# Score bursts without first-layer units, the bias folded into the score matmuls, and a ring of ten activation buffers

## The reference

```python
x = x + attention(layernorm(x))      # 8 heads of 16 channels, 768 x 768 scores
t = t + ffn(layernorm(t))            # t: the same tokens
# attention: softmax(q k / 4 + time_bias[tk - tq] + part_bias[nk - nq]) v, causal in the time
att = att + bias_t + bias_p
att = jnp.where(causal, att, -jnp.inf); att = softmax(att); y = (att @ v) @ Wo
# ffn: two scaled copies of x (top-2 of 8 gate probabilities, normalised), all 8 experts
top_p = top_p / sum(top_p)
for i in range(2):
    h = gelu(einsum('btd,edf->ebtf', x * top_p[..., i:i+1], W1) + b1)
    out = out + einsum('ebtf,efd->btd', h, W2) + b2_sum
```

## Time and profile before

| what | value |
|---|---|
| median of 3 runs | 2730.64 us |
| profiled execution | 2739.47 us, its span 2737.6 us |
| TensorE busy | 2377.7 us (87%), granted clock 0.957 |
| ScalarE busy | 1695.3 us (62%) |
| VectorE busy | 1469.6 us (54%) |
| GpSimd busy | 1089.9 us (40%) |
| first second-layer unit starts (end of the prologue) | 228.5 us |
| last round | 2656.8 to 2737.6 us, 80.8 us |

### The profile page before, as it was taken

One profiled execution on the slowest core, in us unless ns is written; L12 is line 12 of the kernel. 1 busy time (PEld: TensorE's weight loads), 2 busy tenths in 40 slices (PEclk: granted clock), 3 DMA queues, 4 the chain that ended last, 5 costly groups with the idle time before them and its releaser, 6 DMA issues.

```text
span 2737.6 us, 57322 instructions
## 1 busy us (share of the span) xinstructions
PE 2377.7 (87%) x18611; PEld 2127.1 (78%) x18611; DVE 1469.6 (54%) x4157; ACT 1695.3 (62%) x2788; POOL 1089.9 (40%) x1054
## 2 busy tenths in 40 slices
PE   1567989899898989989899898989989898998989
PEld 0347878788887878888787878878887787888878
DVE  7536365444735545474554636544573554547454
ACT  2125656675675666666566665667566566756667
POOL 6004244343433434343343424434352443434347
PEclk9678999999999999999999999999999999999999
DMA  2411212040221303022030212203022120302200
GB/s 34 73 38 25 28 28 34 7 52 7 31 28 20 42 7 43 13 34 28 10 49 10 31 25 34 28 8 51 10 28 28 24 38 7 44 12 34 28 10 7
DMA packets 62802, 74.34 MB, mean 27 GB/s; under 512 B 16192, under 2 KB 43744, under 8 KB 62432
## 3 DMA queue, kind: packets, MB, share of 16 engines
q1 hardware_dynamic: 62528, 70.68, 18.4%
HBM read 11.19 MB, written 6.29 MB: 6 GB/s over the span
## 4 chain that ended last, share of the span: by engine, by line
PE 57%; DVE 17%; issue 13%; ACT 9%; DMA 2%; POOL 1%; SPq 1%; DVEq 0%; POOLq 0%; ACTq 0%
PE acc L904 15%; PE wide L827 6%; PE narrow L844 6%; PE zps L893 6%; ACT z L504 5%; PE wide L830 5%; DVE wide L656 5%; PE zps L895 4%; PE zps L894 4%; PE wide L811 4%; DVE h L727 2%; PE wide L865 2%; PE wide L851 1%; DMA stack<-stack 1%; DVE maxes L656 1%
## 5 line engine op out<-in xcount | busy, mean ns | idle before, releaser
L445 POOL TENSOR_TENSOR hsum<-h 128x384 f32<-128x384 f32 x1024 | 1030.2, 1010 | 1491.9 <-ACT h L533 1477.3
L727 DVE TENSOR_TENSOR h<-zps,ratio_b 128x384 f32<-128x384 f32 x1024 | 561.8, 555 | 921.1 <-PE zps L895 917.3
L532 ACT ACTIVATE h<-zps,b_col 128x384 f32<-128x384 f32 x1024 | 594.3, 580 | 662.4 <-DVE h L727 637.1
L904 PE MATMUL acc<-w,hsum 128*128 128x128 f32 x6144 | 867.3, 278 | 1.4 <-DVE outt L736 1.2
L904 PEld LDWEIGHTS acc<-w,hsum 128*128 128x128 f32 x6144 | 850.2, 195 | 2.2 <-POOL hsum L445 1.7
L533 ACT ACTIVATE h<-h,b_col 128x384 f32<-128x384 f32 x1024 | 620.7, 606 | 0.0
L893 PE MATMUL zps<-x_hi,w_lo 128*128 128x384 f32 x1024 | 426.5, 416 | 100.7 <-ACT h L532 57.6
L656 DVE CUSTOM_DVE_ANT_0 wide<-wide,query_table 128x768 f32<-128x768 f32 (+5 forms) x768 | 461.6, 649 | 46.7 <-PE wide L811 44.0
L827 PE MATMUL wide<-stack 128*128 128x256 f32 (+3 forms) x1280 | 374.7, 323 | 69.9 <-ACT z L504 33.9
L504 ACT ACTIVATE z<-wide 128x896 f32<-128x896 f32 (+2 forms) x384 | 345.3, 918 | 95.1 <-PE wide L830 94.3
L894 PE MATMUL zps<-x_lo,w_hi 128*128 128x384 f32 x1024 | 353.4, 345 | 0.0
(11 more groups left out here) (110 smaller groups left out, 1609.2 us busy)
## 6 DMA issues: line engine op xcount, KB each, us to landing
stack<-halves SPq DMA_DIRECT2D x512, 96.0 KB
x_in<-in_x SPq DMA_DIRECT2D x136, 48.0 KB, 2.4
out_dram<-outt SPq DMA_DIRECT2D x256, 24.0 KB, 1.6
stack<-stack SPq DMA_DIRECT2D x128, 6.0 KB
z<-in_L_ffn_W SPq DMA_DIRECT2D x8, 256.0 KB, 4.2
stack<-max_rows SPq DMA_DIRECT2D x64, 12.0 KB
bias_rows<-w_hi SPq DMA_DIRECT2D x1, 192.0 KB
bias_rows<-w SPq DMA_DIRECT2D x1, 192.0 KB
```

What stands on the lines that cost most here:

```text
L445: pool.tensor_tensor(hsum[:, m % NHS, :], h0[:, m % 2, :], h1[:, m % NH1, :], ALU.add).then_inc(hsum_ready, 1)
L532: act.activation(h0[:, m % 2, :], zps[m % 2][:, 0:CT], ACT.Gelu, bias=b1_col[:, j:j + 1]).then_inc(h0_ready, 1)
L727: vec.tensor_tensor(h1[:, m % NH1, :], zps[m % 2][:, 0:CT], ratio_b[:, c * CT:(c + 1) * CT], ALU.mult).then_inc(z1_ready, 1)
L904: ins = pe.matmul(acc[:, n * P:(n + 1) * P], hsum[:, k % NHS, n * P:(n + 1) * P], w2[:, j, :], start=(j == 0 and n == 0), stop=(j == UNITS ...
```

## The change

- **Schedule.** Slots 20 to 25 and 41 to 46 get no first-layer unit; twelve other slots (`DOUBLE`) get two. So the first layer leads by 4 up to slot 5, by 10 after slots 16 and 37, and by 4 again after each burst. The twelve score steps of a group are spread two a slot over a burst. `query`, `key`, `value` move to slots 1, 2, 3 (from 2, 2, 4), the first maxima to slot 6 (from 8), `mix` to `project` to 47..51 (from 44..49), `split` of chunk 1 to slot 62 (from 60).
- **Ring.** `hsum` is gone: GpSimd adds `h0` into `h1` in place. `h1` has ten places; `ring_places()` gives the 64 units turns of 10, 9, 9, 9, 9, 9, 9 places. VectorE's product of unit m now waits for the second-layer unit m - BACK[m]; BACK is 9 for m = 0 to 8 and for every m from 19 on, 10 for m = 10 to 18, and 64 for m = 9.
- **Bias.** `qst` has a row block for each of the 8 heads with 768 + 384 columns; three products of halves take 48 rows, the bias tables and their one-hot keys rows 48 to 126, the maxima row 127. So one matmul gives scores with bias, for maxima and for scores; VectorE's maximum is a plain `tensor_reduce`. `rows` keeps the high half alone. Each `stack` step has six DMAs instead of five, `rows` eight instead of two.
- **Gate.** top-2 weights by tanh of half the difference of the two largest logits, instead of exp and sums.
- **Prologue.** Other bias tables, W1 staged in `w2`'s place earlier.

```diff
-NHS = 4
-STACK_DMAS = 5
+BURSTS = (20, 41)
+BURST = 6
+DOUBLE = (6, 8, 10, 12, 14, 16, 27, 29, 31, 33, 35, 37)
+RING = 10
...
+    plan += maxima(0, (6, 7, 8, 9, 10, 11, 12, 13, 14, 15, 16, 16)) + [(17, "rows", 0)]
...
+FIRSTS = [0 if any(b <= k < b + BURST for b in BURSTS) else 2 if k in DOUBLE else 1 for k in range(UNITS)]
+def ring_places():
+    turns = next([RING] * n + [RING - 1] * ((UNITS - RING * n) // (RING - 1)) for n in range(UNITS)
+                 if (UNITS - RING * n) % (RING - 1) == 0)
+    return [n for turn in turns for n in range(turn)]
+PLACE = ring_places()
+BACK = [next(d for d in range(1, UNITS + 1) if PLACE[m - d] == PLACE[m]) for m in range(UNITS)]
...
+                m = LAG
                 for k in range(UNITS):
                     steps(k, False)
-                    if k + LAG < UNITS:
-                        unit(this, k + LAG)
...
+                    for _ in range(FIRSTS[k]):
+                        if m < UNITS:
+                            unit(this, m)
+                        elif following:
+                            unit(following, m - UNITS)
+                        m += 1
                     after(this, k)
...
-                    for n, (q, k) in enumerate(((0, 2), (1, 2), (0, 3), (1, 3))):
+                    for n, (q, k) in enumerate(((0, 2), (1, 2), (0, 3))):
...
+                    for n, q in enumerate((0, 1, 0)):
+                        sp.dma_start(qst[n * HD:(n + 1) * HD, h, TOK:QW].bitcast(F32),
+                                     halves[rows, q, HALF:TOK]).then_inc(stack_loaded[hh], 16)
...
                 pool.wait_ge(h1_ready, r.at(UNITS, m + 1))
-                pool.wait_ge(hsum_used, r.at(UNITS, m + 1))
-                pool.tensor_tensor(hsum[:, m % NHS, :], h0[:, m % 2, :], h1[:, m % NH1, :],
+                pool.tensor_tensor(h1[:, PLACE[m], :], h0[:, m % 2, :], h1[:, PLACE[m], :],
...
-                    act.activation(gate_e[:, :, :], shifted[:, :, :], ACT.Exp).then_inc(gate_exped, 1)
+                    act.activation(gate_t[:, :], gate_d[:, :], ACT.Tanh, scale=0.5).then_inc(gate_exped, 1)
...
-                        ins = vec.tensor_tensor_reduce(w[:, at:at + n], w[:, at:at + n],
-                                                       query_table[:, h, TOK - n:TOK], 1.0, -3e38, ALU.add, ALU.max,
...
+                        ins = vec.tensor_reduce(maxes[:, hh * TILES + i:hh * TILES + i + 1], w[:, at:at + (i + 1) * P], AX.X, ALU.max)
...
-                vec.wait_ge(hsum_ready, r.at(UNITS, m + 1))
-                vec.tensor_tensor(h1[:, m % NH1, :], zps[m % 2][:, 0:CT], ratio_b[:, c * CT:(c + 1) * CT],
+                vec.wait_ge(hsum_used, r.at(UNITS, m + 1 - BACK[m] + UNITS))
+                vec.tensor_tensor(h1[:, PLACE[m], :], zps[m % 2][:, 0:CT], ratio_b[:, c * CT:(c + 1) * CT],
...
-                        ins = pe.matmul(w[:, at:at + q1 - q0], key_hot[:, g, :], bias_rows[:, hh, q0 - i * P:q1 - i * P],
-                                        start=False, stop=True)
+                        shift = HALF if i >= HT else 0
+                        ins = pe.matmul(w[:, at:at + q1 - q0], kst[:, hh, i * P:(i + 1) * P],
+                                        qst[:, g * GH + hh, q0 + shift:q1 + shift], start=True, stop=True)
```

More of the change, by code:

```diff
@@ L50, in maxima, with scores @@
         return [(slot, "maxima", (g, n // 3, n % 3)) for n, slot in enumerate(slots)]
+    def scores(g, at):
+        return [(at + n // 2, "scores", (g, n // 3, n % 3)) for n in range(3 * GH)]
     plan = [(-5, "stats", 0), (-5, "seed", 0), (-4, "root", (0, 0)), (-4, "root", (0, 1)), (-4, "root", (0, 2)),
-            (-3, "scale", (0, 0)), (-2, "scale", (0, 1)), (0, "turn", 0), (2, "query", 0), (2, "key", 0), (4, "value", 0)]
-    plan += [(4, "stack", (0, hh)) for hh in range(GH)]
-    plan += maxima(0, (8, 9, 10, 11, 12, 13, 14, 15, 16, 17, 18, 20)) + [(22, "rows", 0)]
@@ L56, in attention_plan @@
-    for hh in range(GH):
-        plan += [(26, "scores", (0, hh, n)) for n in range(3)] + [(26, "stack", (1, hh))]
-    plan += [(27, "mix", (0, 0)), (28, "mix", (0, 1))]
[L59 to L62, removed]
@@ L63, in attention_plan @@
-    plan += [(50, "stats", 1), (51, "seed", 1), (51, "root", (1, 0)), (52, "root", (1, 1)), (52, "root", (1, 2)),
+            (-3, "scale", (0, 0)), (-2, "scale", (0, 1)), (0, "turn", 0), (1, "query", 0), (2, "key", 0), (3, "value", 0)]
+    plan += [(3, "stack", (0, hh)) for hh in range(GH)]
+    plan += maxima(0, (6, 7, 8, 9, 10, 11, 12, 13, 14, 15, 16, 16)) + [(17, "rows", 0)]
+    for n, step in enumerate(scores(0, BURSTS[0])):
+        plan.append(step)
+        if n % 3 == 2:
+            plan.append((step[0], "stack", (1, n // 3)))
@@ new lines, in attention_plan @@
+    plan += [(27, "mix", (0, 0)), (28, "mix", (0, 1))]
+    late = [(30, "sums", 0), (32, "divide", 0)] + maxima(1, (28, 29, 29, 30, 31, 32, 33, 34, 34, 35, 36, 37))
+    plan += sorted(late, key=lambda step: step[0]) + [(38, "rows", 1)]
+    plan += scores(1, BURSTS[1])
+    plan += [(47, "mix", (1, 0)), (48, "mix", (1, 1)), (49, "sums", 1), (50, "divide", 1), (51, "project", 0), (51, "load", 1)]
+    plan += [(51, "stats", 1), (52, "seed", 1), (52, "root", (1, 0)), (53, "root", (1, 1)), (53, "root", (1, 2)),
@@ L586, in _ @@
+            vec.wait_ge(tables_low, 2)
             vec.sem_inc(z1_ready, 2)
@@ L741, in after @@
                         residual(r, 1)
-            rounds(vec, attention, unit, after, last=("stats", "seed", "root", "scale", "rows"), prepare=prepare)
+            rounds(vec, attention, unit, after, last=("stats", "seed", "root", "scale"), prepare=prepare)
         @block.tensor
```

369 lines of the change are left out of this document (170 added, 199 removed).

## The result

| what | before | after |
|---|---|---|
| median | 2730.82 us (2728.61 to 2734.73, 4 runs) | 3014.41 us (3006.76 to 3018.9, 4 runs) |
| ratio of the two | | 1.1034, 95% interval 1.1008 to 1.106 |
| span of the profiled execution | 2737.6 us | 3016.9 us |
| prologue / a round / last round | 228.5 / 161.9 / 80.8 | 203.5 / 180.5 / 105.8 |
| granted clock | 0.957 | 0.881 |

A forecast was written before the change was run, and what follows sets the result against it. Maxima slots bound by TensorE and VectorE, score steps by TensorE with ScalarE just behind, plain slots by ScalarE. 2739.5 + 63 (fifteen rounds at +4.2) - 44.5 + 17 = 2775 us profiled; median 2770, range 2695 to 2850.

The forecast's parts named there:

- The ring's wait: Slots 16 to 19 and 37 to 40: products wait for second-layer units ahead in program order, +9.9 us a round.
- The loop: Second-layer unit, VectorE's product, ScalarE's gelu and back to TensorE: 2.76 us a slot instead of 1.19.
- the clock: Rival, chance 0.12, listed beside the forecast; the median was put at 2770 instead of 2766 for the clock.
- Bias matmuls and bursts: -8.0 us a round: Score steps without bias matmuls, spread over bursts: gains of 4.1 and 3.9 us in the two bursts of a round.
- free product: Case in the bursts: if unit 29's product need not wait for second-layer unit 20, 2.6 us more gain each.
- Gate: -2.1: Gate in each round: two table loads of 1.28 us and four small VectorE operations go, -2.1 us.
- First heads' DMA and double slots: Maxima slots, per round: +1.8 us for TensorE's wait for the first heads' DMA, +1.8 for maxima in double slots.
- Prologue: -44.5: Before the rounds: score steps 32 us earlier, score parts 6 shorter, `gate` and `weigh` 6.5 shorter; bounds -30 and -58.
- twelve bias DMAs to 43: In the prologue: 1.8 MB at 0.1 MB/us, done at 43 us, first head at 47 instead of 86.8.
- Last round: +17: Last round, with no attention to fill it: 91.3 us against 73.8 by the same count; bounds +8 and +22.
- The ring's wait is hidden: Rival, chance 0.21 in whole or part: the six ring slots run at 1.19 us, total 2607 us.
- The score part gains nothing: Rival, chance 0.07: exps wait 0.4 us each slot, reductions take 0.2 longer a step; +8 us a round, 2890.

The follow-up runs named there:

- experiment 2: The changed kernel with a ring of eleven places instead of ten, output tiles moved into `res` and `mixed`, same schedule: 2713.53 us, ratio 0.9941.
- experiment 4: The changed kernel with five unread filler matmuls behind each of second-layer units 16 to 18 and 37 to 39 in the rounds: 2965.34 us, ratio 1.0856.
- plain kernel: The changed kernel with the slot plan of before and one first-layer unit in every slot (no bursts, lead 4): 2687.44 us, ratio 0.9842.
- experiment 10: The changed kernel with eleven ring places, filler matmuls in the layer norm and split, and Wo's DMAs behind W1's: 2674.79 us, ratio 0.9786.
- experiment 7: The plain kernel with two unread filler matmuls behind each score step of the rounds: 2636.8 us, ratio 0.9657.
- experiment 6: The changed kernel with exp in place of tanh in the gate, which brings the two table loads back: 2993.7 us, ratio 1.0965.

## Why the prediction was wrong

The forecast was 2775 for the profiled execution, which took 3018.9. Of the 244 us, 15 x 14.4 = 216 lie in the rounds, 19.5 in the prologue (203.5 against 184), 8 in the last round (105.8 against 98). Of the 14.4 us a round, 3.8 are the ring's and 10.6 lie in what the rest of the round was to save.

**The ring's wait: right in mechanism, too small.** The loop's 2.76 us were 2.78; the product waits for `acc` in slots 15 to 20 and 36 to 41. The forecast gave it 9.9 and, in the bursts, twice the 2.6 by which the first exp comes later: 15.1. The changed kernel loses 20.1 in those stretches and 18.9 a round net against eleven places. Experiments 2 and 4 put at most 14.7 of it down to the loop and the late start. That this is so near 15.1 is partly luck: the loop slots cost 7.6 at full clock and not 9.9, and what follows 7.1 and not 5.2, with some half clock in it. The rest is the clock. I had given it a chance of 0.12 as an alternative to the loop, and it was its consequence: the loop leaves TensorE busy for only 1.46 of the 2.78 us of a turn (slots 18 and 19 in a round without half clock), and with fillers, busy 4.67 of 5.57 us from unit 17 to 19, the turns keep 1.00 and 2.78 us (experiment 4), where at 0.50 a turn takes 3.93. It also reaches what follows: the first exp at +7.55. The 4 us that the forecast adds for the clock (2766 to 2770) come from no row and no run shows them; the runs showed a clock of 0.881 in place of 0.957, of which at least 5.4 us a round came in the stretches of the ring and the bursts (experiment 4).

**"Bias matmuls and bursts: -8.0 us a round": this is the step that failed.** Without the ring's share the forecast round is 4.2 - 15.1 = 10.9 below before; with eleven places it is 0.3 below. The bursts themselves came out as worked out: with a free product 23.1 and 26.6 us for the stretches from 19 and from 40, where 25.2 - 2.6 and 29.7 - 2.6 were expected. Wrong was what they were set against. I credited the first-layer units that a burst lacks at TensorE's 0.53. They must be done elsewhere: between units 5 and 20 the bursts' kernel takes 33.6 us, the plain one 23.3, for five first-layer units, a transpose of the maxima and two score steps. Of these 10.3 us the forecast had 5.8: 2.7 for the five units, 1.3 for the double slots and 1.8 for the first head's DMA. The burst then returns 9.5 of the 10.3 (20 to 26: 12.4 against 21.9); over the second group, 26 to 51, the balance is -3.2, over the layer norm and the head of the round, 51 to 64 and 0 to 5, +3.7. The clock has a smaller share: in experiment 10, at 0.97, the round is 159.4 instead of 161.6, so 2.2 of the missing 10.6 us are clock and 8.4 are not, though a part of those lies in the terms below.

In the plain kernel the clock is the larger matter. I took the bias matmuls' time for time saved at the same clock; plain against before is 1.6 a round, and with the clock mostly held it is 5.0 (experiment 7).

**Gate: -2.1 was 0 or a loss.** The trace has no table load ahead of tanh: the gate's 15 (L516) and 15 of the 46 at the gelu (L532, 31 at L540 now), 1.28 us each, are gone. But the loads were not on the path: with them back the kernel is no slower, and without them VectorE's multiplications take 0.7 us a round more (experiment 6).

**First heads' DMA and double slots: about right.** TensorE waits 1.31 us for the first head (forecast 2.1), and in the first group a pair of a double and a single slot takes 4.4 (forecast 4.2).

**Prologue: -44.5 was -25.** The failed link is "twelve bias DMAs to 43". The size was right, 6 x 192 and 6 x 96 KB, but they went at 0.06 MB/us and not at the 0.1 of `stack` (before the change the five DMAs of a head, 390 KB, are issued every 3.3 us, from 1207.33, 1210.66 and 1214.04): SyncE issues them from 26.9 until 56.9, and Wo's behind them:

```profile
stack<-z SPq DMA_DIRECT2D x6, 192.0 KB
stack<-z SPq DMA_DIRECT2D x6, 96.0 KB
...
26.93 0.72 SPq L347 DMA_DIRECT2D stack<-z  x1
...
51.05 3.79 SPq L347 DMA_DIRECT2D stack<-z  x1
54.88 1.99 SPq L348 DMA_DIRECT2D stack<-z  x1
56.91 8.54 SPq L351 DMA_DIRECT2D wo_pad<-in_L_conv_Wo  x8
71.12 1.94 PE L791 MATMUL wide<-stack 127*128 127x128 f32 x6 [36.15 <-DMA stack<-halves]
90.29 3.70 ACT L548 CAST w_hi<-w 128x2048 fp32r<-128x2048 f32 x2 [54.48 <-DMA w<-in_L_ffn_W]
```

The first maxima start at 71.1 instead of 47 and W1's copy at 90.3 instead of 70; from the first score step to unit 0 it is then 106.6 us, forecast 105.5.

**Last round: +17 was +25.** Eleven places make it 87.8, so the ring is 18 us of the 25, where the forecast had 9.9 for its loops; the half clock is in these 18 as well (0.89 against 0.97).

**The rivals.** "The ring's wait is hidden" is refuted by the waits (371.5 us) and by experiment 2. "The score part gains nothing" was right in its effect at 0.07, though by the clock and the double slots and not by its two causes. The clock, the score part and the forecast add up; I treated them as excluding each other, and so the range ended at 2850. What stays open: how the 21 us of experiment 6 part between the multiplications and the clock, why the eleven-place kernel keeps its full clock in the bursts, and what sets the clock of a score slot from round to round in experiment 7.

## What to carry to other kernels

Compare the lead with the places of the ring in its shortest turn: one unit of lead beyond them (here 10 over 9) was a closed loop over three engines, and it cost at a stroke (2.78 us a slot against 1.2). Work that is taken from an engine or moved away from it is a gain only if it is set against the slots that receive it, and on TensorE only if the clock survives (0.90 with the bias matmuls and 0.69 without in the score slot of experiment 7): look at the granted clock of the stretch before counting matmuls saved. Where TensorE waits in small pieces for ScalarE, a few idle matmuls into a free buffer are a cheap test of that (51 us in experiment 7).

## What the runs showed that I had not expected

- 48 useless matmuls a round made the plain kernel 1.9% faster (2687.4 to 2636.8); 30 a round in the ring slots made the changed one 1.6% faster (3014.4 to 2965.3).
- A multiplication of 128 x 128 by VectorE took 279 ns alone; with one addition of GpSimd among six of them one took 1.06 us, and the average of all is 400 ns.
- A DMA of 8 rows by 8 heads from SBUF to SBUF held SyncE's issue for 3.8 us (192 KB, from the third on) or 2.0 (96 KB, from the second on); the first two of the row took 0.72 and 0.69, and those of the rounds (96 KB) take 0.65.
